# Half of batches 1 to 5's probabilities turned on VectorE and moved through scratch memory in DRAM; x normalised on GpSimd

## What is computed

```python
xn      = layernorm(x)                                    # over the last axis
theta_x = einsum('ld,bdt->btl', theta_w, ctx) + theta_b
phi_x   = einsum('ld,bdt->blt', phi_w, xn) + phi_b
p       = softmax(einsum('btl,bls->bts', theta_x, phi_x)) # 512 x 512 per batch
g_x     = einsum('ld,bdt->btl', g_w, xn) + g_b
t_x     = einsum('bts,bsl->blt', p, g_x)
h       = relu((t_x - mean) * rsqrt(var + eps) * gamma + beta)
x       = x + tanh(g_xattn) * (einsum('ol,blt->bot', out_w, h) + out_b + ctx)
n       = layernorm(x)
hid     = silu(bitlinear(n, w1)) * bitlinear(n, w2)
x       = x + tanh(g_ffn) * bitlinear(hid, w3)
# bitlinear: rmsnorm, rows rounded to 8 bits, weights to -1, 0, 1 times their mean absolute value
```

## Time and profile before

| | |
|---|---|
| median of 3 runs | 300.76 us (300.74 to 300.8) |
| profiled execution | 300.9 us, span 298.9 us |
| PE busy | 294.7 us, 99% of the span |
| DVE, ACT, POOL busy | 241.2 us (81%), 197.2 us (66%), 193.8 us (65%) |
| last chain | PE 93%, ACT 4%, DMA 2% |
| DMA | 37.00 MB, mean 124 GB/s |

### The profile page before, as it was taken

How to read it: one execution, slowest core, us unless ns; L and a number is a source line. 1 busy time by engine, 2 the same in 40 slices (tenths; PEclk the granted TensorE clock), 3 DMA queues, 4 the chain that set the end, 5 groups by cost and what they waited for, 6 DMA issues and landing times.

```text
span 298.9 us, 4419 instructions
## 1 busy us (share of the span) xinstructions
PE 294.7 (99%) x1350; PEld 160.1 (54%) x1350; DVE 241.2 (81%) x541; ACT 197.2 (66%) x347; POOL 193.8 (65%) x293
## 2 busy tenths in 40 slices
PE   8999999999999999999999999999999999999996
PEld 5765757575757566644444444444444444444444
DVE  3799889796969797899888788887986896876872
ACT  1389898989989877699954736455465547445720
POOL 3351789594949286666988778586786786665610
PEclk9999999999999999999999999999999999999999
DMA  7999970094320002010326366144324342561456
GB/s 252 411 418 414 405 281 3 16 385 163 140 71 0 0 3 35 0 38 0 70 52 77 83 127 114 40 110 106 72 70 106 73 111 64 102 109 50 93 101 183
DMA packets 52936, 37.00 MB, mean 124 GB/s; under 512 B 43056, under 2 KB 43696, under 8 KB 51888
## 3 DMA queue, kind: packets, MB, share of 16 engines
q1 hardware_dynamic: 52624, 36.45, 42.5%
q10 hardware_dynamic: 288, 0.27, 0.3%
HBM read 22.02 MB, written 4.19 MB: 88 GB/s over the span
## 4 chain that ended last, share of the span: by engine, by line
PE 93%; ACT 4%; DMA 2%; SPq 0%; DVE 0%; issue 0%
PE bank L1149 37%; PE bank L1167 17%; PE bank L1093 9%; PE bank L1071 7%; PE bank L1108 5%; PE bank L1086 4%; PE bank L1058 4%; PE bank L1048 4%; PE bank L1037 4%; ACT wq L492 2%; DMA c_sb<-ctx_in_dram 2%; PE bank L1180 1%; ACT prob L539 1%; ACT probT L535 1%; PE bank L1120 0%; PE bank L1116 0%
## 5 line engine op out<-in xcount | busy, mean ns | idle before, releaser
L1149 PE MATMUL bank<-wq,stage 128*128 128x512 bf16 x512 | 113.3, 379 | 0.0
L1149 PEld LDWEIGHTS bank<-wq,stage 128*128 128x128 bf16 x512 | 50.1, 98 | 61.5 <-issue 2.3
L816 DVE SCALAR_TENSOR_TENSOR stage<-bank,s,stage 128x512 f32<-128x512 f32 x64 | 47.5, 744 | 22.2 <-PE bank L1149 18.2
L573 ACT ACTIVATE xn<-stage 128x1024 f32<-128x1024 f32 x31 | 32.8, 1057 | 46.2 <-DVE stage L816 46.2
L565 ACT ACTIVATE stage<-bank,s 128x512 f32<-128x512 f32 x64 | 43.2, 681 | 16.3 <-PE bank L1149 14.3
L1167 PE MATMUL bank<-wq,prob 128*128 128x512 bf16 x224 | 50.5, 379 | 0.0
L428 POOL TENSOR_SCALAR stage<-stage,hsc 128x1024 f32<-128x1024 f32 x30 | 33.4, 1123 | 20.3 <-DVE hsc L847 20.3
L346 POOL TENSOR_SCALAR prob<-prob,rsum 128x512 f32<-128x512 f32 x29 | 19.6, 694 | 30.9 <-DVE rsum L718 30.9
L821 DVE TENSOR_REDUCE m<-stage 128x1 f32<-128x1024 f32 x31 | 37.7, 1216 | 0.8
L1167 PEld LDWEIGHTS bank<-wq,prob 128*128 128x128 bf16 x224 | 21.9, 98 | 26.4
L1071 PE MATMUL bank<-ph,th 128*128 128x512 f32 x96 | 36.0, 487 | 0.0
(11 more groups left out here) (117 smaller groups left out, 434.3 us busy)
## 6 DMA issues: line engine op xcount, KB each, us to landing
stage<-w1t_dram SPq DMA_DIRECT2D x4, 1024.0 KB, 11.5
stage<-w2t_dram SPq DMA_DIRECT2D x4, 1024.0 KB, 14.6
stage<-w3t_dram SPq DMA_DIRECT2D x4, 1024.0 KB, 5.8
x<-x_dram SPq DMA_DIRECT2D x7, 512.0 KB, 10.8
c_sb<-ctx_in_dram SPq DMA_DIRECT2D x7, 512.0 KB, 6.3
out_dram<-stage SPq DMA_DIRECT2D x14, 256.0 KB, 2.3
pc<-pack_c_dram SPq DMA_DIRECT2D x1, 640.0 KB, 15.5
x<-x_dram SPq DMA_DIRECT2D x2, 256.0 KB, 3.4
```

Of the source, the lines that this page charges most:

```text
L573: A.activation(junk, h_sb[t % 2][:, half * HF:(half + 1) * HF], ACT.Square, accum_out=ssq[:, half:half + 1]).then_inc(sq_done, 1)
L816: V.scalar_tensor_tensor(h_sb[k][:, c * 512:(c + 1) * 512], up_banks(n)[1][:, :], s12[:, u % 2, 1, k:k + 1], sil[n % 3], ALU.mult, ALU.mul ...
L1149: last = mm(bank[:, :], turned[:, row:row + P], wq[:, at:at + 512], start=q == 0, stop=q == KI - 1)
```

## The change

For batches 1 to 5 (`by_blocks`), keys 256 to 511 of the probabilities no longer go through TensorE and ScalarE. VectorE turns them in 32x32 blocks (`turn_blocks`, two instructions of 128x512) into `blocks`, one DMA of 512 KB writes `blocks` to the DRAM tensor `spill`, and four DMAs of 128 KB read it back into `placed`, each to 32 partitions, which puts the blocks in their places. `values(i, 2)` and `values(i, 3)` of these batches read `placed` and are made one step later, behind `phi(i+2)`.

```diff
+        spill_v = spill.rearrange("(q b) (k r) -> k b q r", b=32, k=4)
...
+            def by_blocks(i):
+                return 1 <= i <= B - 3
...
-            return banks[(4, 5, 6, 2)[c] if i == 0 else (0, 1, 0, 2)[c]]
+            return banks[(4, 5, 6, 2)[c] if i == 0 else (0, 1, 4 if by_blocks(i - 1) else 0, 2)[c]]
...
+            def move_blocks(i):
+                sp.wait_ge(blocks_ready, 2 * i)
+                if i >= 2:
+                    sp.wait_ge(blocks_moved, 64 * (i - 1))
+                sp.dma_start(spill[:, :], blocks[:, :]).then_inc(blocks_out, 16)
+                sp.wait_ge(blocks_out, 16 * i)
+                sp.wait_ge(tx_done, i)
+                for k in range(4):
+                    sp.dma_start(placed[32 * k:32 * (k + 1)], spill_v[k]).then_inc(blocks_moved, 16)
...
+            def turn_blocks(i, k):
+                if k == 0:
+                    dve.wait_ge(pnorm_ready, 4 * i + 4)
+                    if i >= 2:
+                        dve.wait_ge(blocks_out, 16 * (i - 1))
+                V.transpose(blocks[:, :].rearrange("p (s k c r) -> p k c s r", s=4, k=2, c=TC)[:, k],
+                            prob[:, i % 2, :, (2 + k) * P:(3 + k) * P].rearrange("p c (s r) -> p c s r", r=32))\
+                    .then_inc(blocks_ready, 1)
...
             def values(i, c):
-                pe.wait_ge(pT_ready, 4 * i + c + 1)
+                if by_blocks(i) and c >= 2:
+                    pe.wait_ge(blocks_moved, 64 * i)
+                else:
+                    pe.wait_ge(pT_ready, turn_no(i, c) + 1)
```

The normalised x of batches 2 to 7 is made on GpSimd (`x_norm` there, as (x + (-mean)) times the root), late in the step before. Of these batches' four multiplications of p with 1/sum, GpSimd keeps two in batches 1 to 5, and ScalarE makes the other two, right behind `theta_high`. The weight pieces are joined in pairs, in three slots a step:

```diff
-                for c in range(chunks):
+                for c in range(2 if by_blocks(i) else chunks):
...
-                2: ((M, 0, 6), (M, 0, 7), None, (M, 1, 0), (M, 1, 1), (M, 1, 2), (M, 1, 3)),
+                1: ((M, 0, 3, 1), None, (M, 0, 4)),
+                2: ((M, 0, 6), None, (M, 1, 0)),
+                3: ((M, 1, 2), (M, 1, 4), (M, 1, 6)),
+                4: ((S, 0, 0), (S, 0, 2), (S, 0, 4)),
+                5: ((S, 0, 6), (M, 2, 0), (M, 2, 2)),
...
+                if i >= 3:
+                    relu(i - 3)
+                if i == 1 or by_blocks(i - 1):
+                    normalise(i - 1)
```

More of the change, by code:

```diff
@@ L207, in gated_cross_attention_bitffn, with piece @@
         block = ctx.enter_context(nc.Block())
-        def piece(k, p):
+        def piece(k, p, n=1):
             at = (k % 2) * WCOLS + p * WP
-            return stage[:, at:at + WP]
+            return stage[:, at:at + n * WP]
         @block.sync
@@ L451, in _ @@
                     tx_root(i - 2)
+                if i + 1 < B:
+                    x_norm(i + 1)
+                if i == 6:
+                    prep_root(0)
                 if i == 2:
@@ L513, in slot @@
                 if weight_work[i][n] is not None:
-                    step, k, p = weight_work[i][n]
-                    step(k, p)
+                    step, *what = weight_work[i][n]
+                    step(*what)
             def theta_high(i):
@@ L598, in _ @@
                     p_copy(i - 1, 1)
+                if i >= 2:
+                    slot(i, 2)
                 exp(i, 0)
-                if i >= 1:
+                whole = i >= 1 and not by_blocks(i - 1)
+                if whole:
                     p_copy(i - 1, 2)
                 exp(i, 1)
-                slot(i, 5)
-                if i >= 1:
+                if i == 1:
+                    slot(i, 2)
+                if whole:
                     p_copy(i - 1, 3)
                 exp(i, 2)
-                if i >= 2:
-                    relu(i - 2)
-                slot(i, 6)
                 if i == B - 1:
+                    relu(B - 3)
                     center(1)
@@ L854, in down, with first_steps @@
                     .then_inc(xo_ready, 1)
[L856 to L868, removed]
+            def first_steps(i):
+                if i == 1:
+                    sum_inverse(0)
+                x_stats(i + 1, 0)
+                low_part(i, th, b_th, 0, th_ready, thl_ready)
+                if i == 0:
+                    low_part(0, ph, b_ph, 1, ph_ready, phl_ready)
+                x_stats(i + 1, 1)
+                if i == 1:
+                    low_part(1, ph, b_ph, 1, ph_ready, phl_ready)
+                    weight_abs(0)
+                row_max(i, 0)
+                if i == 0:
+                    x_norm(1)
+                else:
+                    residual(1)
+                row_max(i, 1)
+                if i == 1:
+                    weight_abs(1)
+                row_max(i, 2)
+                row_max(i, 3)
+                if i == 0:
+                    residual(0)
+                else:
+                    weight_abs(2)
@@ L1065, in scores @@
                     pe.wait_ge(phl_ready, i + 1)
-                elif c == 2 and i >= 1:
+                elif c == 2 and i >= 1 and not by_blocks(i - 1):
                     pe.wait_ge(exp_done, 4 * i + 1)
@@ L1108, in out_proj, with mean_mm @@
                 mm(b_out(i, o)[:, :], out_w[:, o * P:(o + 1) * P], hn[:, :], start=True, stop=True).then_inc(out_done, 1)
-            def mean_mm(i, weight=None):
+            def mean_mm(i):
                 pe.wait_ge(lmean_ready, i + 1)
@@ L1190, in _ @@
                 theta(i)
+                phi(i)
                 if i in (4, 7):
                     weight_total({4: 1, 7: 2}[i], i)
+                if by_blocks(i - 2):
+                    values(i - 2, 2)
+                    values(i - 2, 3)
                 if i >= 3:
                     out_proj(i - 3, 0)
-                phi(i)
-                if i >= 3:
-                    mean_mm(i - 2, {4: 1, 7: 2}.get(i))
+                g(i)
                 if i >= 3:
                     out_proj(i - 3, 1)
-                g(i)
-                if i == 2:
-                    mean_mm(0)
+                if i >= 2:
+                    mean_mm(i - 2)
+                whole = i >= 1 and not by_blocks(i - 1)
                 if i >= 1:
```

246 lines of the change are left out of this document (140 added, 106 removed).

## The result

The changed kernel takes 301.77 us (median of 7 runs, 301.41 to 302.37), the kernel before 300.74 in the same session: 1.0034 of it, 95% interval 1.0024 to 1.0044. It is slower by 1.0 us, where 3.1 us less were forecast, and lies outside the range that was given (296.2 to 300.6). The profiled execution took 302.16 us, with a span of 300.4.

The account below looks back on a forecast made before the run. TensorE, busy 99% of the span, was the bound. Transposes -4.4, hole -0.25, step 1 +0.35, batch 1 +0.8, batch 3 +0.3 gave -3.2 us; median 297.6, with step 7's +0.1 297.7, range 296.2 to 300.6.

Parts of the forecast that it names:

- The likeliest case: The whole kernel: all terms as summed, 297.7 us, its own range 296.9 to 299.0, chance 0.46.
- The saving: TensorE in five steps: ten groups of four transposes go, at 0.44 us each, 4.4 us less.
- rival (c): VectorE becomes the bound: block turns of 2.5 us each delay `mean_mm` by 2 us in five steps; 307, chance 0.05.
- Batch 1, +0.8: Step 3: TensorE waits for batch 1's last read behind a queue full of weights; +0.8 us, bounds 0.35 and 2.2.
- Batch 3, +0.3: Step 5: batch 3's transfers stand behind a w3 load that waits for ScalarE; +0.3 us, bounds 0 and 1.7.
- Step 1, +0.35: Step 1: a joined weight piece on ScalarE delays the copy of quarter 3; +0.35 us, between 0 and 1.05.
- The hole of step 2: Step 2: about 0.25 us that TensorE lost behind ScalarE's copy go, as two weight pieces fewer stand there.
- Step 7, +0.1: Step 7: ScalarE has six sign pieces instead of three, its first exp just in time; +0.1 us if anything.
- rival (a): All five trips: transfers are hidden everywhere; 296.8 us, or 296.3 if step 1 is free too; chance 0.2.
- (b): Trips are late: each 2.5 us longer, batches 1 and 3 stall that much more; 302.7 us, chance 0.16.
- (d): Many small waits on the fuller ScalarE, VectorE and GpSimd: 0.4 us in each of six steps; 300.1, chance 0.13.

Follow-up runs that it names:

- e3: Changed kernel with the last quarter of w2 loaded behind batch 1's transfers instead of ahead of them; 300.76 us.
- e4: Changed kernel with batch 3's transfers issued ahead of the first quarter of w3 and the context tile of batch 5; 303.89 us.
- e6: Changed kernel with SyncE's order: context tile of batch 5, then batch 3's transfers, then the first quarter of w3; 299.74 us.
- e7: Changed kernel with weight loads moved behind the transfers of batches 1, 3 and 4, and context tiles of batches 5 and 6 early; 298.33 us.
- e8: e7 with t_x statistics before the feed-forward scales in step 7, and quarter 3's copy before the joined weight piece in step 1; 298.32 us.
- e1: Changed kernel with products reading un-turned probabilities, so TensorE waits for no transfer; block turns and all DMAs still run; 301.42 us.
- e2: e1 with the five writes and twenty reads not issued at all, nor VectorE's wait for the writes; 298.00 us.
- e5: Changed kernel with no batch by blocks: all probabilities turned on TensorE, no transfers, new orders, joined weight pieces and x on GpSimd kept; 306.51 us.
- e10: The changed kernel itself measured once more, nothing changed; 302.07 us.

## Why the prediction was wrong

The likeliest case had the two late trips in the right places, and nothing else of TensorE's waits for transfers; the step that failed is the time at which the writes land behind a full queue, in the terms of batch 1 and batch 3. Beside them the terms of steps 1 and 7 were too small.

- **The saving** of 4.4 us is there: steps 4 and 6 take 14.72 and 14.42 us, against 14.65 forecast. The products from `placed` take what those from `probT` take (1.72 us for two, 1.98 behind a wait).
- **The block turns** take 1.31 us for two, 0.66 each, against 0.69 forecast. They sit in VectorE's slack: rival (c) is wrong. In step 3 they waited for GpSimd, as forecast, 2.9 us (timeline of VectorE):

```profile
31.96 1.31 DVE L772 STREAM_TRANSPOSE blocks<-prob 128x512 f32<-128x512 f32 x2 [0.47 <-ACT prob L589]
...
45.86 1.30 DVE L772 STREAM_TRANSPOSE blocks<-prob 128x512 f32<-128x512 f32 x2 [2.94 <-POOL prob L385]
```

- **Batch 1, +0.8: this term failed** (+2.5 found). The blocks were ready at 33.3, about as forecast, and most of the queue had run empty at 38.8, where I had the write's last byte at 38.7. But I let it land at 39.5, and it landed at 41.0. Windows of half a microsecond of the changed kernel (last two: DMA share, GB/s):

```profile
38.00:38.50 0.50, 0.50 (x4) 0.26 (x2) 0.47 (x3) 0.50 (x3) 0.50 (x2) 1.00 0.98 397
38.50:39.00 0.50, 0.50 (x3) 0.25 (x2) 0.50 (x3) 0.50 (x3) 0.50 (x2) 1.00 0.53 213
39.00:39.50 0.50, 0.50 (x3) 0.38 (x2) 0.50 (x2) 0.27 (x2) 0.50 (x1) 1.00 0.08 29
39.50:40.00 0.50, 0.50 (x3) 0.25 (x2) 0.50 (x1) 0.00 (x0) 0.50 (x1) 1.00 0.06 25
40.00:40.50 0.50, 0.50 (x3) 0.26 (x2) 0.50 (x2) 0.38 (x1) 0.50 (x2) 1.00 0.06 25
40.50:41.00 0.50, 0.50 (x3) 0.25 (x2) 0.50 (x2) 0.50 (x3) 0.50 (x1) 1.00 0.00 0
```

  From 39.0 to 40.5 the share is 0.06 to 0.08, one engine of sixteen, and 25 to 29 GB/s are a sixteenth of 400. The packet records of the trace agree: the last eight packets of the write, 4096 bytes each, ran one behind the other from 39.29 to 40.54, while nothing else moved. One of the sixteen was 1.5 us behind the others, and the write had landed when the last part had. It was behind before the write's turn came: from 35.2 to 36.7 one engine was still at the 8192-byte packets of a weight load, and the others at the 2048-byte packets of the tile behind it. Why it lagged, no run shows. The trace of the kernel before had the same end of the queue, which the 2 us window 42 to 44 hides and my figure of 42.75 leaves out:

```profile
43.00:43.50 0.50, 0.50 (x3) 0.22 (x2) 0.00 (x0) 0.50 (x2) 0.22 (x1) 1.00 0.16 61
43.50:44.00 0.50, 0.50 (x3) 0.26 (x2) 0.32 (x2) 0.50 (x3) 0.05 (x1) 1.00 0.06 25
44.00:44.50 0.50, 0.50 (x3) 0.26 (x2) 0.47 (x2) 0.50 (x2) 0.50 (x1) 1.00 0.06 25
```

  The last read then took 2.94 from its issue, where I had some 2.4. The sum for the start of step 3 was wrong too: 41.9 - 1.7 - 0.88 - 0.25 + 0.35 is 39.4 and not 39.1 (39.5 found), so my own terms gave a stall of 0.2 to 0.6 and not of 0.6 to 1.0. e3 takes a weight load from ahead of the write, and the wait is gone.
- **Batch 3, +0.3: this term failed too** (+2.0 found). The quarter of w3 was issued 6.84 us into the step (6.55 forecast), the write landed at 15.8 (14.7), the last read at 20.05 (18.3). Here it isn't one engine at the end. The queue moved at 274 to 295 GB/s between 66 and 72 us, where loads had run at 389, and within that at 90 and 111, with half of the sixteen engines' time unused:

```profile
67.50:68.00 0.50, 0.50 (x5) 0.45 (x4) 0.50 (x1) 0.50 (x2) 0.00 (x0) 1.00 0.51 90
68.00:68.50 0.50, 0.50 (x4) 0.26 (x3) 0.50 (x3) 0.50 (x1) 0.21 (x1) 1.00 0.48 111
```

  The write's packets begin at 69.6 us, so this stretch lies in the two loads ahead of it. Its cause is open. e4, e6 and e7 settle that the loads ahead are what makes the write late: with none ahead it lands in 2.6 us, and step 5 has no wait for a read.
- **Step 1, +0.35** (bounds 0 and 1.05): +0.77 found, and only the earlier start of the step made the first row of the table look right. Of it 0.35 us is a wait that I had not: `turn_p` of step 1 for GpSimd's multiplication (at 19.44, on TensorE's timeline). The rest is the late copy, as walked: e8 makes that copy before the weight piece, and the step is 0.43 shorter. The hole of step 2 gave back 0.07, not 0.25.
- **Step 7, +0.1: failed**, +0.8. I had walked ScalarE's side, whose first exp came as said, and not VectorE's, where `prep_scale` stands ahead of `tx_gamma`. But e8 takes that wait away and gains nothing, so it is one of several paths of about that length. What the 0.8 is made of stays open.
- **Missing altogether:** what stands behind a trip on SyncE. In the changed kernel it costs 0.7 us of ScalarE's time only; e1 shows it at 2.65 us, once TensorE is no longer late itself.
- **What is left without the stalls.** e7 has neither of the two waits. That is the case of rival (a), 296.8, but e7 took 298.33. By the step lengths the 1.5 us more are 0.9 in step 7, 0.4 in step 1 and 0.2 in the hole of step 2. So the forecast would have been too low without the late trips as well.
- **The rivals.** (b) had the right kind of loss with its turning point, "1.6 us more per trip, then the gain is gone": steps 3 and 5 each lost 1.7 us more than forecast, and the gain is gone. But I gave it 0.16, and took as its cause that the small transfers themselves are slow. They aren't: 2.6 us for the write on an empty queue, against my 3.0. Its sign, late reads in all five steps, didn't come either. (a) fails by the two stalls, and (d) by e2 and e7, whose steps 4 to 6 take 14.4 to 14.7 us. Both failed trips are those for which the prediction itself found no slack. The Trainium skill, page "DMA: Bandwidth & Descriptors", section "Anatomy of one DMA", fits its 2.0 us plus bytes over 436 GB/s to DMAs issued from GpSimd; the estimates by it are 3.2 us for the write and 2.3 for a read, and SyncE's took 2.6 on an empty queue and 2.4 to 2.9 here. In place of my 2.95 and 2.0 they would have added up to 0.55 to a stall, not 0.3. They say nothing of a write behind 1.5 to 2.6 MB, 7.7 to 9.2 us here. The trap of the Trainium skill's page "VectorE: DVE Perf Modes", section "The three transpose paths", did not show: the reads in runs of 1 KB land in 2.4 to 2.9 us.

## What to carry to other kernels

A trip through memory costs its issues, its landings, and all that stands in the same queue, on both sides: what is ahead of it delays it, and not only by bytes over rate: here by 1.5 us more at the end of a long queue, which half-microsecond windows of the trace before show and 2 us windows hide. What is behind it waits while the issuing engine waits for the landing. Before such a trip is put into a stream of loads, write down for every load its deadline and what it waits for, and order the queue by that: here the order alone was worth 3.4 us (301.77 to 298.33), more than three quarters of the 4.4 that the trip was to save. And when a sum has terms with no slack, their error is one-sided: a stall forecast at 0.3 became 2.0, and it could not have become less than nothing.

## What the runs showed of the hardware

- At the end of a long DMA queue one engine of sixteen was busy 1.5 us longer than the rest (share 0.06 to 0.08 from 39.0 to 40.5 us); the kernel before, the changed kernel and e10 all show it.
- A 512 KB write to DRAM lands 2.6 us after its issue on an empty queue, in four of five trips of e7. In the changed kernel it took 7.7, 8.0 and 9.2 us with 1.5 to 2.6 MB of loads ahead (batches 1, 3 and 4).
- After TensorE had stood 2.1 us in e5, the granted clock was 0.50 for 3.4 us, and two products took 2.00 us instead of 1.02. After its waits of 2.4 and 1.9 us in the profiled run of the changed kernel the granted clock stayed at 1.00.
- A pass of x (128x512) on GpSimd, with an operand for the addition and one for the multiplication, took 0.76 to 1.32 us in the changed kernel, a multiplication of the same size 0.69 to 0.70 each time. Why was not separated.
- A turn of 128x512 f32 in 32x32 blocks on VectorE, SBUF to SBUF, took 0.67 to 0.72 us (ten of them in the changed kernel).
